# Softmax denominators summed with a matrix of ones and inverted as rows, in a two-layer attention kernel

## The reference

```python
# layer 0 (inner width 64)
g, theta, phi = g_w x + g_b, theta_w x + theta_b, phi_w x + phi_b
y = softmax(theta^T phi) g                 # softmax over the 4096 keys
x = W_w y + W_b + x
# layer 1 (width 128)
q, k, v = Wq x + bq, Wk x + bk, Wv x + bv
x = x + softmax(q^T k / sqrt(128)) v
```

## Time and profile before

| | |
|---|---|
| median of 3 runs | 3556.16 us (3555.7 to 3556.31) |
| the profiled execution: its own time | 3554.52 us |
| its span in the profile | 3552.7 us |
| mean granted TensorE clock | 0.992 |
| matmuls (PE) busy | 3476.9 us, 98% |
| weight loads (PEld) busy | 1999.6 us, 56% |
| VectorE (DVE) busy | 2360.3 us, 66% |
| ScalarE (ACT) busy | 1494.4 us, 42% |
| GpSimd (POOL) busy | 2500.8 us, 70% |

### The profile page before, as it was taken

One profiled execution on the slowest core, in us unless ns is written; L12 is line 12 of the kernel. 1 busy time (PEld: TensorE's weight loads), 2 busy tenths in 40 slices (PEclk: granted clock), 3 DMA queues, 4 the chain that ended last, 5 costly groups with the idle time before them and its releaser, 6 DMA issues.

```text
span 3552.7 us, 45057 instructions
## 1 busy us (share of the span) xinstructions
PE 3476.9 (98%) x12740; PEld 1999.6 (56%) x12740; DVE 2360.3 (66%) x3029; ACT 1494.4 (42%) x2017; POOL 2500.8 (70%) x1142
## 2 busy tenths in 40 slices
PE   7999999999999999999999999999999999999999
PEld 4445466666555446666655455666665544566665
DVE  4555577777655557777765555777776555677775
ACT  4445433333444543333345454333334445333333
POOL 4888666666788866666678886666668888566665
PEclk9999999999999999999999999999999999999999
DMA  1000000000000000000000000000000000000000
GB/s 42 19 12 18 27 10 22 12 21 15 19 17 17 18 23 15 16 18 18 13 19 18 18 16 22 16 15 21 15 19 13 18 18 16 18 13 14 13 7 15
DMA packets 34032, 61.66 MB, mean 17 GB/s; under 512 B 5280, under 2 KB 5920, under 8 KB 33568
## 3 DMA queue, kind: packets, MB, share of 16 engines
q1 hardware_dynamic: 33824, 59.23, 5.5%
HBM read 42.44 MB, written 16.78 MB: 17 GB/s over the span
## 4 chain that ended last, share of the span: by engine, by line
PE 90%; DVE 5%; issue 3%; ACT 1%; POOL 0%; SPq 0%; DVEq 0%; DMA 0%; ACTq 0%
PE acc_out L432 22%; PE acc_out L429 14%; PE rough L385 13%; PE scores L407 9%; PE scores L410 7%; PE scores L412 6%; PE scores L416 6%; PE scores L413 6%; DVE piece_max L730 2%; DVE rparts L757 2%; PE rough L367 2%; PE acc_out L373 1%; PE acc_out L452 1%; PE acc_out L441 1%; PE acc_out L447 1%
## 5 line engine op out<-in xcount | busy, mean ns | idle before, releaser
L271 POOL TENSOR_TENSOR sums<-sums,probs 128x1024 f32<-128x1024 f32 x886 | 2117.8, 2390 | 706.2 <-ACT probs L648 566.0
L730 DVE TENSOR_REDUCE piece_max<-rough 128x1 f32<-128x512 f32 x2024 | 1309.5, 684 | 645.1 <-PE rough L385 644.7
L648 ACT ACTIVATE probs<-probs 128x1024 f32<-128x1024 f32 x512 | 542.0, 1059 | 1220.7 <-DVE probs L747 1218.0
L432 PE MATMUL acc_out<-probs,v_vals 128*128 128x512 f32 x2048 | 963.4, 593 | 0.0
L747 DVE TENSOR_TENSOR probs<-scores,shift_rows 128x1024 f32<-128x1024 f32 x512 | 625.4, 1221 | 462.3 <-PE scores L416 448.6
L655 ACT ACTIVATE probs<-scores 128x1024 f32<-128x1024 f32 x512 | 524.5, 1024 | 692.2 <-PE scores L410 690.3
L429 PE MATMUL acc_out<-probs,g_vals 128*64 128x512 f32 x2048 | 549.7, 617 | 0.0
L432 PEld LDWEIGHTS acc_out<-probs,v_vals 128*128 128x128 f32 x2048 | 384.2, 189 | 285.7 <-issue 247.2
L412 PE MATMUL scores<-qry_a,k_hi 128*128 128x512 f32 x1024 | 532.9, 520 | 0.0
L407 PE MATMUL scores<-qry_a,phi_a 128*128 128x512 f32 x1024 | 449.4, 439 | 0.0
L410 PE MATMUL scores<-qry_b,phi_b 128*128 128x512 f32 x1024 | 404.5, 395 | 0.0
(11 more groups left out here) (86 smaller groups left out, 2117.2 us busy)
## 6 DMA issues: line engine op xcount, KB each, us to landing
x_q<-x SPq DMA_DIRECT2D x32, 256.0 KB, 2.7
x_res<-x SPq DMA_DIRECT2D x32, 256.0 KB, 3.0
mid<-mid_new SPq DMA_DIRECT2D x32, 256.0 KB, 2.2
x_q<-mid SPq DMA_DIRECT2D x32, 256.0 KB, 2.8
x_res<-mid SPq DMA_DIRECT2D x32, 256.0 KB, 3.2
out<-result SPq DMA_DIRECT2D x32, 256.0 KB, 2.3
x_kv<-x SPq DMA_DIRECT2D x24, 256.0 KB, 2.8
probs<-x SPq DMA_DIRECT2D x2, 1024.0 KB, 6.5
```

What stands on the lines that cost most here:

```text
L271: eng.tensor_tensor(sums[:, parity], sums[:, parity], probs[:, s % P_BUFS], ALU.add).then_inc(s_plus, 1)
L432: last = mm(acc_out[:, parity], cols(v_vals, tile, KT), p, start=tile == 0, stop=tile == TILES - 1)
L648: nc.scalar.activation(probs[:, s % P_BUFS], probs[:, s % P_BUFS], ACT.Exp, scale=SCALES[1]).then_inc(s_whole, 1)
L730: nc.vector.reduce_max(piece_max[:, t, c:c + 1], src, AX.X).then_inc(s_reduced, 1)
```

## The change

The denominators come from one matmul with a 128 x 128 matrix of ones as stationary operand and `total` as moving operand. It puts the denominators of all 512 queries, as rows that are the same in every partition, straight into PSUM. VectorE inverts them in four pieces of 128 x 128 into `rrow`, two in step 6 and two in step 7. The rounding, the remainder, ScalarE's eight diagonals and TensorE's two matmuls with `ones_r` go. In layer 0 the output projection is moved from step 10 to step 8 and takes the sums undivided; its result is divided in step 9 and finished, in place, in step 10. In layer 1 the division moves from step 9 to step 8 and reads `o_sb` and `rrow`, both in SBUF. In the turn the projection goes to another PSUM bank, ahead of the denominators.

```diff
-RDEN_AT = 8
-OUT_AT = 10
-FINISH_AT = (11, 9)
+RECIP_AT = (6, 7)
+OUT_AT = 8
+NORM_AT = (9, 8)
+FINISH_AT = (10, 9)
...
                 pe.wait_ge(s_fold, g + 1)
-                for t in range(SUB):
-                    last = mm(acc_out[:, parity, 2 * t:2 * t + 2], total[:, t * P:(t + 1) * P], ones[:, 0:2],
-                              start=True, stop=True)
-                last.then_inc(s_den, 1)
-
-            def reciprocal_rows(g, parity):
-                pe.wait_ge(s_rdiag, 2 * g + 2)
-                mm(acc_out[:, parity], ones_r[:], rdiag[:, 0], start=True, stop=False)
-                mm(acc_out[:, parity], ones_r[:], rdiag[:, 1], start=False, stop=True).then_inc(s_rden, 1)
-
-            def out_projection(g, parity):
-                pe.wait_ge(s_norm, g + 1)
-                mm(acc_out[:, parity], wt_out[:], o_sb[:], start=True, stop=True).then_inc(s_wy, 1)
+                mm(acc_out[:, parity], ones[:], total[:], start=True, stop=True).then_inc(s_den, 1)
+
+            def out_projection(g, place):
+                mm(place, wt_out[:], o_sb[:], start=True, stop=True).then_inc(s_wy, 1)
...
                         if s == OUT_AT and layer == 0:
-                            out_projection(g, parity)
+                            pe.wait_ge(s_recip, SUB * g + SUB)
+                            out_projection(g, acc_out[:, parity])
...
-                    if s == RDEN_AT and st.prev is not None:
-                        reciprocal_rows(st.g - 1, 1 - st.parity)
...
+                    if st.turn:
+                        pe.wait_ge(s_y, st.g + 1)
+                        out_projection(st.g, scores[:, 0, 0:QB])
                     denominators(st.g, st.parity)
-                    reciprocal_rows(st.g, st.parity)
-                    if st.layer == 0:
-                        out_projection(st.g, st.parity)
...
-            def reciprocal_diag(g, part):
-
-                act.wait_ge(s_rparts, 2 * g + part + 1)
-                for t in range(SUB):
-                    last = scaled(rdiag[:, part, t * P:(t + 1) * P], idt, rd(rparts[:, part, t:t + 1]))
-                last.then_inc(s_rdiag, 1)
...
-            def reciprocals(g, parity):
+            def reciprocal(g, parity, t):
+
                 dve.wait_ge(s_den, g + 2)
-                den = acc_out[:, parity, 0:2 * SUB].rearrange("p (t c) -> p t c", c=2)[:, :, 0:1]
-                nc.vector.reciprocal(rcol[:].unsqueeze(2), den).then_inc(s_rcol, 1)
-                dve.wait_ge(s_rcol, g + 1)
-                nc.vector.tensor_copy(rparts[:, 0], rcol[:]).then_inc(s_rparts, 1)
-                dve.wait_ge(s_rparts, 2 * g + 1)
-                nc.vector.tensor_tensor(rparts[:, 1], rcol[:], rd(rparts[:, 0]), ALU.subtract).then_inc(s_rparts, 1)
...
+                at = slice(t * P, (t + 1) * P)
+                nc.vector.reciprocal(rrow[:, at], acc_out[:, parity, at]).then_inc(s_recip, 1)
+
+            def normalise(layer, g, nth, parity, wy):
+
+                dve.wait_ge(s_recip, SUB * g + SUB)
                 if layer == 0:
                     dve.wait_ge(s_wy, nth + 1)
                     dve.wait_ge(s_mid, 16 * nth + 16)
-                    src, dst, bias = acc_out[:, parity], mid_new[:, parity], OUT_B
+                    src, dst = wy, mid_new[:, parity]
                 else:
-                    dve.wait_ge(s_norm, g + 1)
-                    src, dst, bias = result[:], result[:], V_B
-                nc.vector.scalar_tensor_tensor(out=dst, in0=src, scalar=bias, in1=x_res[:],
+                    dve.wait_ge(s_stored, 16 * nth + 16)
+                    src, dst = o_sb[:], result[:]
+                nc.vector.tensor_tensor(dst, src, rrow[:], ALU.mult).then_inc(s_norm, 1)
+
+            def finish(layer, g, nth, parity):
+
+                dve.wait_ge(s_xres, 16 * g + 16)
+                dve.wait_ge(s_norm, g + 1)
+                at, bias = (mid_new[:, parity], OUT_B) if layer == 0 else (result[:], V_B)
+                nc.vector.scalar_tensor_tensor(out=at, in0=at, scalar=bias, in1=x_res[:],
                                                op0=ALU.add, op1=ALU.add).then_inc(s_done, 1)
```

More of the change, by code:

```diff
@@ L128, in build @@
         o_sb = sb("o_sb", [P, QB])
-        rcol = sb("rcol", [P, SUB])
-        rparts = sb("rparts", [P, 2, SUB], F32R)
-        rdiag = sb("rdiag", [P, 2, QB], F32R)
+        rrow = sb("rrow", [P, QB])
         result = sb("result", [P, QB])
@@ L184, in build @@
         s_den = sem("s_den")
[L185 to L188, removed]
+        s_recip = sem("s_recip")
         s_wy = sem("s_wy")
@@ L586, in copy @@
                 return nc.scalar.activation(dst, src, ACT.Identity, bias=bias, scale=scale)
-            def scaled(dst, src, scale):
-                return nc.scalar.activation(dst, src[:], ACT.Copy, scale=scale)
             def take_q_whole(g, layer, src):
@@ L688, in block_program @@
                         probs_shifted(st.nth, s)
-                    if s in (DEN_AT + 1, DEN_AT + 2) and st.prev is not None:
-                        reciprocal_diag(st.g - 1, s - DEN_AT - 1)
                     if st.phi_g:
@@ L710, in block_program @@
                     take_q_hi(1, st.parity, scores[:, 1, 0:QB])
-                if st.ends:
-                    reciprocal_diag(st.g, 0)
-                    reciprocal_diag(st.g, 1)
             def turn(b):
@@ L810, in block_program @@
                         layer, g, nth, parity = before(st)
[L811 to L814, removed]
+                        if s in RECIP_AT:
+                            for t in range(2):
+                                reciprocal(g, parity, 2 * RECIP_AT.index(s) + t)
+                        if s == NORM_AT[layer]:
+                            normalise(layer, g, nth, parity, acc_out[:, parity])
                         if s == FINISH_AT[layer]:
@@ L832, in block_program @@
                     fold(dve, st.g, st.parity)
-                    reciprocals(st.g, st.parity)
-                    normalise(st.layer, st.g, st.nth, st.parity)
+                    for t in range(SUB):
+                        reciprocal(st.g, st.parity, t)
+                    normalise(st.layer, st.g, st.nth, st.parity, scores[:, 0, 0:QB])
                     finish(st.layer, st.g, st.nth, st.parity)
```

## The result

The changed kernel takes 3573.3 us (median of 5, 3572.5 to 3574.54), the kernel before 3555.7 (median of 5). The ratio is 1.0051, with a 95% interval of 1.0040 to 1.0063: slower by 17.6 us, where 19 us less were forecast. The profiled execution took 3573.3 us, with a span of 3571.5.

What follows compares the result with a forecast made beforehand. TensorE's queue of matmuls was taken to bound the kernel. Layer-0 blocks -11, layer-1 blocks -1, turns and end -6.5 gave -19 us: 3535.5 from the profiled 3554.5, or 3537 as median; range 3520 to 3575.

Steps and rivals of the forecast that it cites:

- TensorE's own saving: Matmuls removed and added on TensorE in steps 5 and 8: -0.36 us a block in layer 0, -0.48 in layer 1.
- The reciprocal: VectorE's 128 x 128 reciprocal, not in the trace: taken as 0.95 us, with 0.30 and 1.29 kept for the range.
- The rival with the slow reciprocal: Third piece of step 7, both layers: reciprocal of 1.22 us makes it wait; +17 us, 3573; chance 0.22.
- Step 7 in layer 1: Step 6's 0.52 us wait goes; reciprocals make the shift and third piece of step 7 late, costing 0.67 us.
- The turn: Between layers: shorter way from denominators to `k_hi`, -1.8 us worked out, -1.5 taken for the clock, four times.
- The division in step 8: Layer 1, VectorE: two SBUF operands beside GpSimd lose 0.55 us; counted as 0.15 + 0.15 for step 8's third piece.
- Layer 0's finish: Layer 0, VectorE: finish now reads two SBUF operands, but VectorE idles 1.3 us in each step; no cost counted.
- The second rival: Layer 1, step 8: GpSimd holds the division 1.6 us, not 0.55; 28 us more, 3565; chance 0.04.

## Why the prediction was wrong

The forecast was -19 us and the result +17.6. Step by step:

- **TensorE's own saving: right.** -0.36 a block was forecast in layer 0, and the stretch from step 4 to step 10, which ends ahead of the interval behind the finish, is 0.40 shorter in the block shown and 0.35 in the mean. The new denominators cost 0.86 in both layers.
- **The reciprocal: right.** 0.95 us forecast, 0.90 measured. The rival with the slow reciprocal had named 3573 us, and the kernel lands there, but not by its mechanism: at 0.90 us it does not apply, and the third piece of step 7 in layer 0 does not wait.
- **Step 7 in layer 1: right.** The wait of 0.52 in step 6 goes. The third piece of step 7 was to cost 0.67 over 3.80 and costs 0.54.
- **The turn: right.** To `k_hi` -1.8 us was worked out and -1.8 measured. With an allowance for the clock -1.5 was taken, four times, and the turns gave 5.7 together, 1.4 each; in two of the four the lower clock did last 2 us longer behind `k_hi`.
- **The division in step 8: the step that failed.** It reads: "has a median of 1.31 us against a minimum of 0.75: 0.55 lost on the way [...] It stands ahead of the shift of step 8, where 0.4 to 0.5 us is free, so I count 0.15 + 0.15". The hold is 1.7 us in nearly every block, and the interval of step 8 is 1.50 over its sum, not 0.30. I took the finish's median as the mean of chance meetings. It was the outcome of one fixed rhythm, in another step, and an instruction elsewhere in that rhythm has another hold. Layer 1's blocks came out at about +1.00 in place of -0.03: 28 x 1.03 = 29 us of the 36.6 that the forecast is off.
- **Layer 0's finish: also mis-sized.** "VectorE idles 1.3 us in each of its steps" was put against a hold of nearly 2 us. The interval behind it grew by 0.32 in most blocks: 8 us in all, put at nothing.
- **The second rival** named the mechanism and its full price, 28 us, and got a chance of 0.04 because line 779's median spoke against it. With +28 on the forecast's -19 and 8 for the layer-0 finish it gives +17, and the two profiled executions differ by 18.8.

The trace of the kernel before could have priced the hold. The finish that was taken as the measure, and GpSimd's addition beside it:

```profile
1531.69 1.31 DVE L779 SCALAR_TENSOR_TENSOR result<-result,vec,x_res 128x512 f32<-128x512 f32 x1
```

```profile
1530.06 2.39 POOL L271 TENSOR_TENSOR sums<-sums,probs 128x1024 f32<-128x1024 f32 x1 [1.67 <-ACT probs L648]
```

The addition ends at 1532.45, 0.76 us after the finish has begun, and the finish ends 0.55 behind that: 0.76 + 0.55 = 1.31. The 0.55 is the same (within 2 ns) in all 28 executions that meet an addition. So 1.31 us is no mean. The division, which reads PSUM and is not held, stands ahead of the finish in this step, and two thirds of the addition are over when the finish comes. In the changed kernel the instruction comes 0.55 us into the addition and waits for the rest, 1.84 + 0.55 = 2.39. The prediction also calls line 779 "the only instruction like that beside a busy GpSimd". It is not:

```profile
L737 DVE TENSOR_TENSOR diag<-neg_ident,query_max x64: 691/2454/2720, 52.4 to 3480.2; 128x512 fp32r<-128x512 f32 x64
```

```profile
L759 DVE TENSOR_TENSOR rparts<-rcol,rparts x64: 161/1182/2353, 112.7 to 3544.9; 128x4 fp32r<-128x4 f32 x64
```

Both read two SBUF tiles. The first, of the division's size, has a median of 2.45 us; the second takes up to 2.35 us for four numbers. Even the cast of 2.34 us, which reads one SBUF tile, begins 0.07 us into an addition and ends 0.03 us behind it:

```profile
1517.54 2.39 POOL L271 TENSOR_TENSOR sums<-sums,probs 128x1024 f32<-128x1024 f32 x1 [1.04 <-ACT probs L648]
```

By these rows the wait of 0.52 us in step 6, which the change was to remove, came from such a hold as well.

That GpSimd's instruction holds VectorE's is shown from four sides: by taking an SBUF operand away (2.39 to 0.68 us, -36 us), by shortening GpSimd's instruction (2.39 to 1.30, -32 us), by taking the reciprocals away (hold unchanged), and by the kernel in which the finish came first and the addition was held. The Trainium skill, page "SBUF — State Buffer", section "Who interferes with whom", says that a VectorE instruction with two SBUF inputs contends with a GpSimd instruction that reads SBUF, that the port pair they share is an exclusive lock, and that the order of issue decides who blocks. The rows above agree: the division ends 0.55 us behind GpSimd's addition, and the finish that began first held the addition, 2.83 us in place of 2.39.

For the cast with its one SBUF input only the meeting and the common end are shown; no experiment altered it.

## What to carry to other kernels

When a change moves an operand from PSUM to SBUF, look at what GpSimd runs at that moment: where its additions last 2.4 us, a 0.7 us multiplication can last 2.4, and one operand left in PSUM removes that. Do not price such a hold by the median of another instruction. Lay the two engines' rows side by side and take how much of GpSimd's instruction is left when VectorE's begins: in a fixed rhythm it is nearly the same in every block, and that rest plus 0.55 us gave each held 128x512 instruction here. And list everyone who waits for the late instruction: rough pieces in step 8, a projection or the next step's pieces in step 9. Moving the instruction, or one of its waiters, hands part of the cost to the next (7.3 and 25.5 us gained, where removing the hold gave 36.3).

## What the runs showed of the hardware

- A reciprocal of 128 x 128 from PSUM takes 896 ns and one of 128 x 16 takes 196: (896 - 196) / 112 = 6.25 ns an element, six times the 1.05 ns of ordinary work. The Trainium skill, page "VectorE: DVE Perf Modes", section "First, the fixed hardware budget", gives Reciprocal a repeat count of 8. If each repeat took those 1.05 ns, an element would take an estimated 8.4 ns; the runs do not bear that reading out.
- Writing the reciprocal back to the PSUM bank that it is read from costs 8 ns (904 against 896).
- A VectorE instruction held by GpSimd shows no idle time in the profile: the wait is inside its duration (2.39 us in place of 0.68). A minimum far below the median or the maximum of one line is the sign of it.
- The hold works both ways. A finish that began 0.13 us ahead of GpSimd's addition took 0.73 us, and the addition 2.83 in place of 2.39.
